# Two scan directions in one accumulator, two PSUM banks per instruction and a new order of work, in a four-layer kernel

## What is computed

```python
x = x + conv3x3(gn(x))                        # layer 0
h1 = relu(bn(nin(gn(x))))                     # layer 1
for d in range(4):                            # d % 2: tokens reversed; d // 2: channels flipped
    u, z = split(in_proj(view(h1, d)))        # 256 channels each
    uc = silu(causal_conv(u) + b)
    dtr, B, C = x_proj(uc)
    dt = softplus(dt_proj(dtr) + dt_b)
    h = exp(dt * A) * h + dt * uc * B         # along 1024 tokens, 16 states per channel
    y = sum_n(h * C) + uc * D
    ym += out_proj(y * silu(z))
x = x + relu(bn(nin2(ym / 4 + h1)))
x = x + x * gates(row_means(gn(x)), column_means(gn(x)))   # layer 2, small scans in it
x = x + post(circuit(gn(x) @ pre))            # layer 3
```

## Time and profile before

| | |
|---|---|
| median of 3 runs (lowest, highest) | 13798.05 us (13795.23, 13801.27) |
| the profiled execution | 13793.3 us |
| its span, first to last instruction | 13791.5 us |
| busy: PE, DVE, ACT, POOL | 88%, 91%, 87%, 91% |
| mean granted clock of PE | 0.946 |
| share of time of the DMA queue | 56.8% of 16 engines |

### The profile page before, as it was taken

One profiled execution on the slowest core, in us unless ns is written; L12 is line 12 of the kernel. 1 busy time (PEld: TensorE's weight loads), 2 busy tenths in 40 slices (PEclk: granted clock), 3 DMA queues, 4 the chain that ended last, 5 costly groups with the idle time before them and its releaser, 6 DMA issues.

```text
span 13791.5 us, 184501 instructions
## 1 busy us (share of the span) xinstructions
PE 12088.6 (88%) x68188; PEld 8349.2 (61%) x68188; DVE 12598.5 (91%) x8502; ACT 12052.7 (87%) x18757; POOL 12608.1 (91%) x3786
## 2 busy tenths in 40 slices
PE   7888889898888888888888888888888888888886
PEld 4566666666666666666666666666666666666654
DVE  7999999999999999999999999999999999999985
ACT  6889888889888898888898888888888988889875
POOL 6999999999999999999999999999999999999985
PEclk8999999999999999999999999999999999999987
DMA  5555555555555555555555555555555555555552
GB/s 188 217 222 218 220 213 223 224 213 221 221 217 219 219 217 222 218 219 221 215 222 217 221 220 220 218 216 222 218 223 215 219 217 218 224 215 222 217 200 110
DMA packets 517060, 2965.20 MB, mean 215 GB/s; under 512 B 57818, under 2 KB 57914, under 8 KB 253890
## 3 DMA queue, kind: packets, MB, share of 16 engines
q1 hardware_dynamic: 516162, 2953.40, 56.8%
HBM read 2889.73 MB, written 46.66 MB: 213 GB/s over the span
## 4 chain that ended last, share of the span: by engine, by line
POOL 27%; issue 25%; DVE 18%; ACT 16%; PE 12%; DMA 0%; POOLq 0%; DVEq 0%; SPq 0%; ACTq 0%
POOL ring L983 18%; DVE ring L1469 10%; POOL ring L966 8%; DVE slot L1455 6%; PE work L1481 5%; PE y_acc L1496 4%; ACT L1000 4%; ACT ring L1160 3%; ACT z_t L1069 2%; PE slot L1496 2%; ACT slot L1160 2%; PE y_acc L1481 1%; ACT work L1052 1%; ACT stack L1050 1%; DVE du L1282 1%
## 5 line engine op out<-in xcount | busy, mean ns | idle before, releaser
L983 POOL TENSOR_TENSOR ring<-ring,c_rows 128x2048 f32<-128x2048 f32 x2048 | 9295.3, 4546 | 814.1 <-DVE ring L1469 809.7
L1469 DVE TENSOR_TENSOR_SCAN ring<-ring,slot 128x1024 f32<-128x1024 f32 x2752 | 6251.9, 2281 | 161.9 <-ACT ring L1160 66.4
L1496 PE MATMUL y_acc<-wk,ring 128*128 128x128 f32 x32768 | 4506.5, 285 | 625.6 <-POOL ring L983 592.6
L1496 PEld LDWEIGHTS y_acc<-wk,ring 128*128 128x128 f32 x32768 | 3975.3, 147 | 1431.0 <-POOL ring L983 766.2
L966 POOL TENSOR_TENSOR ring<-du,b_rows 128x1024 f32<-128x1024 f32 x1344 | 3182.1, 2369 | 180.9 <-PE y_acc L1496 77.4
L1469 DVE TENSOR_TENSOR_SCAN ring<-slot,ring 128x1024 f32<-128x1024 f32 x1344 | 3058.3, 2276 | 277.3 <-POOL ring L966 244.6
L1160 ACT ACTIVATE ring<-dt,a_neg 128x1024 f32<-128x1024 f32 x2752 | 3069.7, 1140 | 52.0 <-PE y_acc L1496 42.2
L1455 DVE TENSOR_TENSOR slot<-du,slot 128x1024 f32<-128x1024 f32 x1952 | 2361.8, 1210 | 53.1 <-PE slot L1481 50.0
L1000 ACT ACT_TABLE_LOAD x1825 | 2341.5, 1283 | 32.0
L1069 ACT ACTIVATE z_t<-du_t,b_t 128x128 f32<-128x128 f32 x6400 | 2037.1, 391 | 40.1 <-PE slot L1496 17.5
L1481 PE MATMUL work<-h_new,fused 128*128 128x512 f32 x4096 | 1914.3, 601 | 46.1 <-ACT b_t L1072 30.6
(11 more groups left out here) (178 smaller groups left out, 9800.0 us busy)
## 6 DMA issues: line engine op xcount, KB each, us to landing
c_rows<-cb_rows_scratch SPq DMA_DIRECT2D x2048, 1024.0 KB, 4.6
b_rows<-cb_rows_scratch SPq DMA_DIRECT2D x1344, 512.0 KB, 5.5
x_next<-in_x SPq DMA_DIRECT2D x32, 512.0 KB, 5.6
x_new_scratch<-x_next SPq DMA_DIRECT2D x32, 512.0 KB, 6.7
h_old<-h_new SPq DMA_DIRECT2D x32, 512.0 KB, 3.2
x_old<-x_new_scratch SPq DMA_DIRECT2D x32, 512.0 KB, 7.3
out<-x_old SPq DMA_DIRECT2D x32, 512.0 KB, 3.2
cb_rows_scratch<-stack SPq DMA_DIRECT2D x128, 100.0 KB
```

What stands on the lines that cost most here:

```text
L983: pool.tensor_tensor(pair, pair, c_rows[:, k % CB_BUFS, :, :], ALU.mult).then_inc(prod_ready, 1)
L1469: dve.tensor_tensor_scan(slot, a, b, 0.0, MUL, ADD).then_inc(scan_done, 1)
L1496: ins = pe.matmul(chunk(out_t, j), chunk(x, j), kc("ident"), is_transpose=True, start=start and j % (BANK // P) == 0, stop=stop, skip_grou ...
```

## The change

- The order of the passes becomes (d, h) = (0,0), (1,0), (0,1), (1,1), then the same for directions 2 and 3 (`pass_of`, `parts_of`). Two passes of a half, 32 units, are summed in `y_acc` and taken once, by DVE with `silu(z)`. The ACT copies and the products that added the kept half go. `du`, `dt` and `u_conv` are kept by direction, `stack` and `b_t` get three buffers. Directions 0 and 1 are convolved and projected before the image begins.
- Silu, softplus, the copy of the time step and `dt_u` take both banks in one instruction (`both`, `both_banks`); the planner hands a stream two banks at once for them (`pairs_in`).
- The plain row sums of the norms 1, 2 and 3 come from the instructions that write `x_next` and `x_old` (`accum_out`), one per bank; PE adds the two in `group_mean` with one more product. Of the two passes over the row, `moment` 0 stays for norm 0 alone.
- `KINDS` is new, with 57 D, 48 P and 23 Z units (61, 42 and 25 before); 15 rows of B are kept for P units, 9 before.
- The planner no longer has fixed unit lists: spreads and turns, sums, products, scans, inputs and decays are flows of their own (`unit_flows`) that it merges with the steps by due time. Costs, `LAG` and all `SHIFTS` are new.

The diff, cut to its core:

```diff
-KINDS = ('DPDPDDDDDPZPDPDZ', 'DPDZDPDZDPZPDPDP', 'DDDDDPZPDZDPZDDP', 'DPDPDPZZZPZPDPDP',
-         'DPZPDPZPDPPDZPDP', 'DPDPDPDDDDZZDPDZ', 'DPDPDPDDZZDDDZDZ', 'DPDPDPDDDDZDZPZP')
+KINDS = ('DPZPZDDDZPZPPPZD', 'DDDZDPDZPDPDPDDP', 'DPDPDPDZPPZZDDPP', 'DDPZDDPPPZZZDPDP',
+         'DPZPPDPZDPDPDZDP', 'DDPDDZPZDPPZDPZD', 'DDPDPPDDPDZPDDPD', 'DPDDDPDPPDPDDPDZ')
...
+def pass_of(d, h):
+    return 4 * (d // 2) + 2 * h + d % 2
...
+def unit_flows(kind):
+    if kind not in ("first", "mid", "last"):
+        return {}
+    of = lambda *kinds: [u for u in range(UNITS) if kind_of(u) in kinds]
+    turned = of("D", "Z")[kind != "first":] + [UNITS] * (kind != "last")
+    return {"D": [[("b", u) for u in of("D")], [("scan", u) for u in range(UNITS)]],
+            "G": [[("input", u) for u in of("P")], [("prod", u) for u in range(1, UNITS, 2)]],
+            "P": [[("zturn" if kind_of(u) == "Z" else "spread", u) for u in turned], [("sum", u) for u in range(UNITS)]],
+            "A": [[("decay", u) for u in range(UNITS)]]}
...
-SUM_LATER = 4
-LAG = {"P": 11., "A": 0., "D": 0., "G": 9.5}
+LAG = {"P": 8., "A": 0., "D": 0., "G": 5.5}
...
-    return steps + [step(("silu", of, d, h, c), "A", key(c)) for c in range(2)]
+    return steps + [step(("silu", of, d, h), "A", both(key(0), key(1)))]
...
+        def both_banks(w):
+            of = work[:, :].rearrange("p (c t) -> p c t", c=2)
+            return of if w is bank_of[0] else of[:, ::-1, :]
...
-                        ins = act.activation(half(u_conv[:, d % 2, h, :], c), w, ACT.Silu, bias=kc("conv_b", h, h + 1))
+                        ins = act.activation(by_half(u_conv[:, d % 2, h, :]), both_banks(w), ACT.Silu,
+                                             bias=kc("conv_b", h, h + 1))
...
-                elif k == "take":
-                    p = name[1]
-                    act.wait_ge(sum_done, s * UNITS + (p + 1) * NST)
-                    ins = act.activation(yz[:, p // 4, p % 2, :], y_acc[:, :], ACT.Copy)
...
-                    ins = act.activation(half(x_old, name[1]), w, ACT.Copy)
+                    c = name[1]
+                    ins = act.activation(half(x_old, c), w, ACT.Copy, accum_out=gn_lanes[:, 1, 2 * c:2 * c + 1])
...
-                    ins = dve.tensor_tensor(half(du[:, h, :], c), w, half(u_conv[:, d % 2, h, :], c), MUL)
+                    ins = dve.tensor_tensor(by_half(du[:, d % 2, :]), both_banks(w), by_half(u_conv[:, d % 2, h, :]), MUL)
...
-                    if n == 5 and d % 2:
-                        halves(y_acc, kc("ident"), yz[:, d // 2, h, :], False, False)
                     pe.wait_ge(prod_ready, s * PAIRS + u // 2 + 1)
-                    turn(y_acc, ring[:, u % RING, :], n == 0, n == NST - 1).then_inc(sum_done, 1)
+                    turn(y_acc, ring[:, u % RING, :], u % (2 * NST) == 0, (u + 1) % (2 * NST) == 0).then_inc(sum_done, 1)
...
+    takes = []
+    for p in range(1, PASSES - 1, 2):
+        f, h = p // 4, p // 2 % 2
+        after = [("sum", p * NST + NST - 1)] + ([("silu", "z", f, h)] if p > 1 else [])
+        if not first:
+            after += [("angles",) if f else ("mix", 4, 1)]
+        takes += [step(("take", p), "D", None, after)] + turn_y("this", f, h)
```

More of the change, by code:

```diff
@@ L143, in silu_pair, with conv, gate_z, project @@
             steps += [step((name, d, h, *k, c), "P", key(c), after if not steps else [])]
-    return steps + [step(("silu", of, d, h, c), "A", key(c)) for c in range(2)]
-def operands(d, first=False):
-    steps = []
[L150 to L155, removed]
+    return steps + [step(("silu", of, d, h), "A", both(key(0), key(1)))]
+def conv(d, h):
+    return silu_pair("u", d, h, "conv_in", [(k,) for k in range(TAPS)])
+def gate_z(f, h, after=()):
+    return silu_pair("z", f, h, "z", [()], after)
+def project(d):
+    steps = []
     for c in range(2):
@@ L164, in timestep @@
 def timestep(d, h):
+    b = [("dt", d, h, c) for c in range(2)]
     steps = []
     for c in range(2):
[L168 to L172, removed]
+        parts = [("part", d, 2, c)] if d > 1 or (d, h) == (0, 0) else []
+        steps += [step(("dt_proj", d, h, c), "P", b[c], parts)]
+    return steps + [step((k, d, h), e, both(*b)) for k, e in (("dt_soft", "A"), ("dt_copy", "A"), ("dt_u", "D"))]
 def turn_du(d, h, last=None):
@@ L456, in wanted @@
             by[("zmul", u, 1)] = u - 1.5
-    by[("take", "before")] = 4
-    for p in range(PASSES - 1):
+    for p in range(1, PASSES - 1, 2):
         by[("take", p)] = p * NST + NST + 4
-    by[("turned_y", "this", 1, 0, 1)] = UNITS - 4
+    by[("silu", "z", 0, 0)], by[("silu", "z", 1, 1)] = UNITS + 2 * NST, UNITS
     want = deadlines(streams, by, pace)
@@ new lines, in pairs_in @@
+def pairs_in(stream):
+    first, last = {}, final_of(stream)
+    for k, x in enumerate(stream):
+        for b in banks_of(x[2]):
+            first.setdefault(b, k)
+    opens = sorted(first.values())
+    lasts = {first[b]: last[b] for b in first}
+    out = dict.fromkeys(range(len(stream)), 0)
+    for k, nxt in zip(opens, opens[1:]):
+        if nxt < lasts[k]:
+            out[k], out[nxt] = 1, 2
+    return out
+def lay(streams, kind, pace, soon_within=SOON, shifts=()):
+    flows = [[(op, e, None, None) for op in flow] for e in "DGPA" for flow in unit_flows(kind).get(e, [])]
+    lines, sides = flows + streams, len(flows)
+    want = wanted(streams, pace, shifts[sides:])
+    cost, last_by = {}, {x: want[x] - SIDE_COST.get(x[0], .3) for x in want}
+    for k, flow in enumerate(flows):
+        for i, (op, *_) in enumerate(flow):
+            last_by[op] = due(op, pace) + (.5 * shifts[k][i] if shifts else 0.)
+    free = dict(LAG if kind in ("mid", "last") else dict.fromkeys("PADG", 0.))
+    end = {("sum", -1): free["P"]}
+    banks, kept, table, pair_of = [0., 0.], [None, None], HOME, None
+    held = [{} for _ in lines]
+    final = [final_of(line) for line in lines]
+    pairs = [pairs_in(line) for line in lines]
+    heads, plan = [0] * len(lines), []
@@ L602, in image_streams @@
     takes = []
-    for p in range(PASSES - 1):
-        f, t, h = p // 4, p // 2 % 2, p % 2
-        after = [("sum", p * NST + NST - 1)]
-        if t == 0 and not first:
-            after += [(("post", 1) if h else ("angles",)) if f else ("mix", 4, 1)]
-        takes += [step(("take", p), "D" if t else "A", None, after)]
-        if t:
-            takes += turn_y("this", f, h)
+    for p in range(1, PASSES - 1, 2):
+        f, h = p // 4, p // 2 % 2
[3 more added lines that the diff above has]
+        takes += [step(("take", p), "D", None, after)] + turn_y("this", f, h)
     zs = []
@@ L635, in count @@
     def count(steps, e):
-        return sum(x[2] == e for x in steps)
+        return sum(x[1] == e and x[3] is not None for x in steps)
     def bases(kind, s):
@@ L647, in numbers @@
         n, out = dict.fromkeys("PADG", 0), {}
-        for x in steps:
-            n[x[2]] += 1
-            out[x[1]] = (x[2], n[x[2]])
+        for name, e, _, after in steps:
+            if after is not None:
+                n[e] += 1
+                out[name] = (e, n[e])
         return out
@@ L943, in step @@
                 ins.then_inc(side["G"], 1)
-            for _, name, e, _, after in before:
+            for name, e, _, after in before:
                 if e == "G":
@@ L1633, in _ @@
             pe.wait_ge(weights_in, 16 * 7)
[L1635 removed]
+            for name, e, bank, after in before:
                 if e == "P":
```

455 lines of the change are left out of this document (225 added, 230 removed), and 96 rows, old and new, of the table SHIFTS.

## The result

The changed kernel takes 14045.6 us (median of 4, 14043.3 to 14048.6) against 13797.6 before: 1.018 times as long, 95% interval 1.0162 to 1.0197. The prediction was 13,580 us and faster, with a range from 13,400 to 13,840: the time moved the other way and lies outside the range.

The account below looks back on a forecast made before the run. DVE and POOL were taken as one equally loaded loop: DVE's 386.1 us plus 30.3 idle, corrected, gives 415 per image instead of 422.4. 32 images -237, front +25, end -2: 13,580 us, range 13,400 to 13,840.

Parts of the forecast that it names:

- What bounds the kernel: DVE and POOL, both busy 91%, form one loop with equal loads; POOL's idle time is almost all waiting for DVE's scans.
- The parts: Per-image work after each part of the change: POOL 407.9 us, DVE 386.1, ACT 348, with some 50 table loads.
- The B loads: SP issues six more loads of B rows for POOL's inputs; costed at nothing, up to 1 us.
- The sum: DVE's 386.1 us of work plus 30.3 idle gives 416.4 per image; two corrections make it 415.
- The corrections: DVE's waits for ACT's time step and for decays and slots halve, -1.3 each; waits for POOL's inputs grow, +1.1.
- The lead-in: Before the first image, direction 1's convolutions and projection come onto the path: +25 us once, bounds +5 and +45.
- The end: Behind the last unit, two passes over rows less: -2 us.
- (a): Rival: POOL alone decides, with only its own waits left: 412 us per image, 13,480 us; chance 0.16.
- (b): Rival: ACT's relief brings nothing and DVE waits longer for the time step: 418 us per image, 13,675; chance 0.12.
- (c): Rival: a full POOL makes every take wait; two more waits per image give 429 us, 14,030; chance 0.13.
- POOL's idle time staying above 14 us: One of two conditions deciding for (c); the other was one more wait of 7 us per image.

Follow-up runs that it names:

- after: The kernel with the whole change as first measured, against the kernel before: 14045.6 us, 1.018 times as long.
- the run that made it longer: Changed kernel with the early store, every merged instruction over both banks issued as two halves again: 13857.6 us, against 13857.2 with merged ones.
- the early store: Changed kernel with one edit: SP stores direction 0's rows ahead of the loads for pair 62, not behind those for pair 63: 13857.2 us, 1.0047 to before.
- measured weights of the kernel before: Kernel before (13795.8 us) with six POOL inputs half wide, 13677.9 us, or twelve DVE products with B half wide, 13747.8: worth 0.57 and 0.26.
- the direct exchange at the old order: Kernel before with six D units made P units, its order kept: +355 us, 14154.0 us, ratio 1.0264.
- exchange runs: P units made D, order kept: kernel before, six 1.0008, three 0.9971 (13755.4 us); changed kernel with the early store, six 1.0047, ten 1.0095 to before.
- their place ahead of a sum: Changed kernel with the early store, PE's spreads and turns right behind a sum issued ahead of it: 13995.5 us, 1.0148 to before.

## Why the prediction was wrong

**What bounds the kernel** was half read. That DVE and POOL form one loop was right. "POOL's idle time is almost all waiting for a scan" was taken to mean that DVE sets the pace. The runs give POOL 0.57 and DVE 0.26 in the kernel before: who waits for whom most did not say whose work counts. (Lines 1317 and 1321, "the small scans of layer 3", are products of layer 2; the 5.4 us stand.)

**The parts** came out. POOL 407.4, DVE 386.3, ACT 349.9 per image; 1555 table loads, 48.6 per image, against "some 50"; `dt_u` 1.20 us; no copy of the accumulator on ACT. The B loads, "nothing, up to 1 us", came to 39.9 us of POOL's waits over 30 images, 1.3 each. The Trainium skill, ScalarE: Activation LUTs, section "What ACT_TABLE_LOAD costs", has a drain beside the load; in after too the next instruction starts 1.30 us after the load does (4811.90 to 4813.20), so the drain was not seen here. ACT's time did not count in the run that made it longer (+100.9 us of work, +0.4 us of time).

**The sum** failed at "if its 30.3 us of idle time stayed, an image would take 416.4". It rose to 43.6. Of the 13.2 us more, the store explains 13.2 - 7.3 = 5.9 of DVE's idle time and 6.5 of the image (429.72 - 423.27). The other 7.3 grew while DVE's work fell by 5.8: its waits for PE's slots went from 1.7 to 11.2 us per image with the early store. From the kernel before to the one with the early store POOL got 439 us more work and DVE 185 less. The measured weights of the kernel before make an estimate of 250 - 48 = +202 us of that and not a gain, and the direct exchange at the old order cost 355. The set-up and the first image add 35.4 + 23.2 = 58.6. Measured are +65.5 and not 261, so something in the new order, the shared accumulator or ACT's relief gives back an estimated 195 us, or more if the exchange run is taken for the loads. Merging is not it (0.4 us), nor, as far as the run with half of `uc * D` tells, PE's shorter work; which part it is was not separated.

So of the 466 us between forecast and result, 188 are the store. The rest, 279 by the spans of the profiled runs, is 261 in images that took 423.3 us where 415 were forecast, 34 in the lead-in and the first image beyond the +25, and -16 at the end.

**The corrections** for ACT's relief (-1.3, -1.3) were worth nothing visible: merging moved the time by 0.4 us. What ACT saves by fewer Z units and takes was not tried alone.

**A moved step and the queues behind it.** The prediction moved the projection of direction 1 ahead of the image and counted its arithmetic. It did not follow the store of direction 0's rows, which stands in SP's program behind the last pair's loads, nor the buffer that both directions share. That wait had no term in the sum; it was +188 us, the largest single cause that a run shows. It was to be seen in the kernel before and the diff: `store_rows(0, ...)` is the last thing before the next image's loads.

**The lead-in** was +25, bounds +5 and +45; up to the first load it measured +35.6, and +14.6 to +23.2 in the first image that no term held: the same chain is met a second time there. The end gave -11.6 where -2 was forecast.

**The rivals.** (a) needed POOL to be fed without a pause; it waits 16.6 us per image even with the early store, 423 instead of 412. (b), ACT's relief worth nothing, was right in its mechanism as far as merging goes, but 418 us was again a sum on DVE's idle time. (c) gave 14,030, 16 us from the result, but by luck, as its mechanism did not happen: the takes cost 6.2 us per image, 6.7 before, though 87 takes waited instead of 30. Its condition "POOL's idle time staying above 14 us" was the useful half: it is 22.5. The Trainium skill, GPSIMD Engine Reference, section on elementwise cycle accounting, would leave such inputs to VectorE. The weights side with it: an input costs 2.37 x 0.57 = 1.35 us of time on POOL and 1.21 x 0.26 = 0.31 on DVE in the kernel before. The exchange runs bear that out for three units, and not for six.

Open: why the fitted orders lose so much when inputs move either way, and what makes PE's spreads late. PE's own length is not it as far as the run with half of `uc * D` tells (142 us less work, +17.5 us with overlapping intervals), their place ahead of a sum made it worse (+138), and the lower clock was not tried.

## What to carry to other kernels

Where two engines of equal load feed each other, measure what a microsecond of each is worth (make a few of its instructions half wide) before an edit trades one for the other; waits alone did not tell it here. When a step is moved ahead in time, walk every queue that its data pass, SP's too, and every buffer that it shares: one DMA issued behind a late wait cost 188 us here. And a statically fitted order is part of the kernel: change the work under it by a little at a time and with the order kept, or the run measures the order.

## What the runs showed that was not expected

- Both engines were 91% busy, and a microsecond was worth 0.57 on POOL and 0.26 on DVE, together 0.83; in the changed kernel POOL's was worth 0.64 at 94% busy. Near-full engines did not count one to one.
- The narrow store of rows (31 partitions, issued at 4832.68) was down 10 us later, while ACT's copy was released at 4842.84; the chain that ended last has single pieces of 10.0 to 10.6 us for it. On a path this store is no small thing, though its issue takes 0.29 us.
